# Attention's maxima pass starts 6 units ahead of the second pass instead of 20

## The chip, the cores and the metric

The kernel runs on one core of one Trainium2 chip. The core has five engines with queues of their own, TensorE (PE in the profile; PEld is its loading of weights), VectorE (DVE), ScalarE (ACT), GpSimd (POOL) and SyncE (SP), and 16 DMA engines. They run side by side and wait for each other on semaphores. The metric is the device time of one execution in microseconds.

## The reference

A block in float32 with a state space layer (two directions, 2 x 2048 tokens, 256 wide) and then a transformer block with causal attention (16 heads of 16) and a mixture of 8 experts. The change lies in the attention alone:

```
q, k = (rope(q), rope(k))
scores = jnp.einsum('bqhd,bkhd->bhqk', q, k) / math.sqrt(hd)
causal = jnp.tril(jnp.ones((Tt, Tt), dtype=bool))
scores = jnp.where(causal, scores, jnp.asarray(-1000000000.0, scores.dtype))
probs = jax.nn.softmax(scores, axis=-1)
attn = jnp.einsum('bhqk,bkhd->bqhd', probs, v).reshape(Bb, Tt, d) @ Wproj
```

with batch 2 and 2048 tokens in each sequence.

## The kernel before

The stages (`project_inputs`, `scan_channels`, `mix_and_qkv`, `attend`, `route`, `run_experts`, `combine`) run one after the other. Inside a stage each engine has its own program, written out in order, with waits on semaphores; nothing schedules them again.

`attend` works through 8 groups of four heads. A group's heads lie on four groups of 32 rows of TensorE, so four score matmuls can run at once. Each group goes through two passes over the causal half of its 2048 x 2048 scores.

The **first pass** finds the largest score of each query. Its piece of work is a *unit*: 128 queries against up to 512 keys, for four heads (`scores1`, line 1561, in two parts of two heads: heads 2 and 3, then 0 and 1). Each head's scores go into one of three PSUM banks (`S1 = 3`); VectorE reduces a bank to one maximum per query (`maxima`, line 1472), and only then is the bank free for the head three places later. 40 units make a group. A unit on the diagonal is narrower (384, 256, 128 or 0 whole columns and one triangle of 128) and ends in a reduction over the triangles (line 1482). A block of 512 queries is a *round*; rounds end with units 3, 11, 23 and 39. After the unit that follows, `turn_max` transposes the round's maxima on TensorE (line 1570, into the first of the three banks), VectorE copies them negated (line 1498), and SyncE writes them with four small DMAs (line 1400) into a spare row of the query tile, counted by `m_in`.

The **second pass** computes the scores again, the other way round, with the maxima subtracted by that extra row. Its piece of work is a *step*: 128 keys against 512 queries (fewer on the diagonal), for four heads, in two halves (`scores2`, line 1582). ScalarE takes the exponential (line 1532; lines 1535 to 1541 on the diagonal), GpSimd clears what lies above the diagonal (line 1438), and TensorE multiplies with the values (`values`, line 1602) one step later. A group has 40 steps; those on the diagonal (0 to 3, 8 to 11, 20 to 23, 36 to 39) are narrower. The first step of a round (0, 4, 12 and 24) waits for the round's `m_in`.

TensorE's program sets the order of both passes. Before step 0 it runs 20 units alone (`LEAD = 20`). Then each step carries one unit, 20 ahead of it: second-pass scores of two heads, first-pass scores of the two other heads, values, and the same again. The last 20 steps carry none.

Of the kernel before, what the change touches and what calls it, by code (L numbers as in the profile page):

```python
# [132 lines left out]
def hold(eng, k):  # L133


    eng.sem_inc(k["passed"], 1)
# [1187 lines left out]
def attend(nc, k, qk, va, attn, load_next):  # L1324
# [7 lines left out]
    GROUPS = B * H // HG  # L1332
    SETS = 2
    PB = 3
    LEAD = 20
    HALF = C // 2
    steps = [(qc, kt) for qc in range(NC) for kt in range(JT * qc + JT)]
    NSTEP = len(steps)


    units = []
    for qc in range(NC):
        whole = [(t, c) for t in range(JT * qc, JT * qc + JT) for c in range(qc)]
        crossed = [(t, qc) for t in range(JT * qc + JT - 1, JT * qc - 1, -1)]
        at = len(whole) if qc < NC - 1 else JT
        units += whole[:at] + crossed + whole[at:]
    assert len(units) == NSTEP
    NUNIT = GROUPS * NSTEP
    ends = [max(st for st, x in enumerate(steps) if x[0] == qc) for qc in range(NC)]
    S1 = 3  # L1350
    with Stage(nc, "attend") as s:
# [29 lines left out]
        @block.sync  # L1381
        def _(sp):
            sp.wait_ge(filled, 2 * SETS + 1)

            def load(n):
                if n >= SETS:
                    sp.wait_ge(s2_mm, (n - SETS + 1) * NSTEP * 2)
                b, g = n // (H // HG), n % (H // HG)
                for h in range(HG):
                    rows = slice((g * HG + h) * HD, (g * HG + h + 1) * HD)  # L1390
                    sp.dma_start(qt[n % SETS][head_rows(h), :], qk[b, 0, rows, :]).then_inc(loaded[n % SETS], 16)
                    sp.dma_start(kt_[n % SETS][head_rows(h), :], qk[b, 1, rows, :]).then_inc(loaded[n % SETS], 16)
                    sp.dma_start(qt[n % SETS][32 * h + HD:32 * h + HD + 1, :], zero[h:h + 1, :]
                                 ).then_inc(loaded[n % SETS], 16)

            def place_max(r):
                n, qc = r // NC, r % NC
                sp.wait_ge(m_rows, r + 1)
                for h in range(HG):
                    sp.dma_start(qt[n % SETS][32 * h + HD:32 * h + HD + 1, qc * C:(qc + 1) * C  # L1400
                                              ].rearrange("r (t q) -> r t q", q=P),
                                 mrows[h * JT:(h + 1) * JT, :]).then_inc(m_in, 16)

            load(0)
            for b in range(B):
                sp.dma_start(vall[:, b * KT:(b + 1) * KT, :, :].rearrange("p t h e -> p t (h e)"),
                             vav[:, b * KT:(b + 1) * KT, :]).then_inc(loaded_v[b], 16)
            for r in range(GROUPS * NC):
                if r % NC == 2 and r // NC + 1 < GROUPS:
                    load(r // NC + 1)  # L1410
                place_max(r)

            for i in range(2):
                sp.wait_ge(stored[i], 16 * NC * (H // HG) // 2)
            load_next(sp)

        @block.gpsimd
        def _(pool):
# [10 lines left out]
            for n in range(GROUPS):  # L1429
                b, g = n // (H // HG), n % (H // HG)  # L1430
                for st, (qc, kt) in enumerate(steps):
                    at = n * NSTEP + st
                    if kt < JT * qc:
# [14 lines left out]
        def round_after(u):  # L1448

            if u < 0 or u >= NUNIT or u % NSTEP not in ends:  # L1450
                return None
            return u // NSTEP * NC + ends.index(u % NSTEP)

# [91 lines left out]
        @block.tensor  # L1545
        def _(pe):
            pe.wait_ge(caps_ok, 1)

            def scores1(u, part):
                n, (t, c) = u // NSTEP, units[u % NSTEP]  # L1550
                if u % NSTEP == 0 and part == 0:
                    pe.wait_ge(loaded[n % SETS], (n // SETS + 1) * HG * 3 * 16)
                w = min(C, (t + 1) * P - c * C)
                for i, h in list(enumerate((2, 3, 0, 1)))[2 * part:2 * part + 2]:
                    v = u * HG + i
                    rows = slice(32 * h, 32 * h + 32)
                    if v >= S1:
                        pe.wait_ge(s1_read, v - S1 + 1)
                    if v % S1 == 0 and turned:
                        pe.wait_ge(m_rows, turned)  # L1560
                    pe.matmul(s1[v % S1][:, 0:w], qt[n % SETS][rows, t * P:(t + 1) * P],  # L1561
                              kt_[n % SETS][rows, c * C:c * C + w], start=True, stop=True).then_inc(s1_mm, 1)

            def turn_max(u, r):

                last = min(u + 1, NUNIT) * HG - 1
                pe.wait_ge(s1_read, last // S1 * S1 + 1)
                pe.wait_ge(m_ok, r + 1)
                hold(pe, k)
                pe.transpose(pm, m[:, :, :].rearrange("p h t -> p (h t)"), k["ident"][:, :]).then_inc(m_turned, 1)  # L1570

            def scores2(at, pair):
                n, (qc, kt) = at // NSTEP, steps[at % NSTEP]
                o = max(kt - JT * qc, 0) * P
                if kt == 0 and pair == 0:
                    pe.wait_ge(m_in, (n * NC + qc + 1) * HG * 16)
                if at:
                    pe.wait_ge(exp_ok, at * 2 - 1 + pair)
                for i in range(2):
                    h = 2 * pair + i  # L1580
                    rows = slice(32 * h, 32 * h + 32)
                    last = pe.matmul(s2[pair][:, i, o:], kt_[n % SETS][rows, kt * P:(kt + 1) * P],  # L1582
                                     qt[n % SETS][rows, qc * C + o:(qc + 1) * C], start=True, stop=True)
                last.then_inc(s2_mm, 1)

            def values(at, half):
                n, (qc, kt) = at // NSTEP, steps[at % NSTEP]
                b, g = n // (H // HG), n % (H // HG)
                o = max(kt - JT * qc, 0) * P
                if half == 0:  # L1590
                    pe.wait_ge(exp_ok, at * 2 + 2)
                    if kt >= JT * qc:
                        pe.wait_ge(kept_ok, n * KT + kt + 1)
                    if kt == 0:
                        pe.wait_ge(loaded_v[b], 16)
                        if n * NC + qc:
                            pe.wait_ge(pv_out, n * NC + qc)
                lo, hi = max(o, half * HALF), (half + 1) * HALF
                if lo >= hi:
                    return  # L1600
                for h in range(HG):
                    last = pe.matmul(pv[32 * h:32 * h + 32, lo:hi], vall[:, b * KT + kt, g * HG + h, :],  # L1602
                                     pb[at % PB][:, h, lo:hi], start=kt == 0 and half == 0,
                                     stop=kt == JT * qc + JT - 1, skip_group_check=True)
                if half == 1:
                    last.then_inc(pv_ok, 1)

            turned = 0
            for at in range(-LEAD, NUNIT):
                u = at + LEAD  # L1610
                if at >= 0:
                    scores2(at, 0)
                if u < NUNIT:
                    scores1(u, 0)
                    if at > 0:
                        values(at - 1, 0)
                if at >= 0:
                    scores2(at, 1)
                if u < NUNIT:
                    scores1(u, 1)  # L1620
                elif at > 0:
                    values(at - 1, 0)
                if at > 0:
                    values(at - 1, 1)
                if round_after(u - 1) is not None:
                    turn_max(u, round_after(u - 1))
                    turned += 1
            values(GROUPS * NSTEP - 1, 0)
            values(GROUPS * NSTEP - 1, 1)

# [709 lines left out]
```

## Time and profile before

| what | value |
|---|---|
| median of 3 runs | 4213.83 us (4213.8 to 4221.78) |
| span of the profiled execution, first to last instruction | 4222.2 us |
| TensorE busy | 3401.3 us, 81% of the span |
| VectorE busy | 2787.7 us, 66% |
| ScalarE busy | 2464.7 us, 58% |
| GpSimd busy | 1886.3 us, 45% |

The profile is of one execution, and gives no time of its own beside the span. It lies 8.4 us above the median and 0.4 us above the slowest of the runs. Busy times are unions of an engine's instructions; ends of matmuls are modelled. Attention runs from 2255.07 to about 3456 us of this span.

### The profile page before, as it was taken

How to read it: one execution, taken by the hardware profiler on the slowest of the kernel's cores; microseconds unless marked ns; L12 is line 12 of the kernel's file. 1: busy time of each engine (PE TensorE's matmuls, PEld its weight loads, DVE VectorE, ACT ScalarE, POOL GpSimd, SP SyncE). 2: the span in 40 equal slices, each digit the busy share in tenths (PEclk: the TensorE clock that was granted, in tenths of full speed). 3: DMA queues.
4: the chain of work that ended last, by engine and by line, in shares of the span. 5: the costliest groups of instructions: out<-in, count | busy, mean ns of one | idle time of the engine just before them, and what ended most of it. 6: DMA issues, size and time to landing. Idle time of an engine off the chain costs nothing. (4 is left out here: it accounts for less than half of the span.)

```text
span 4222.2 us, 69815 instructions
## 1 busy us (share of the span) xinstructions
PE 3401.3 (81%) x22940; PEld 2121.0 (50%) x22940; DVE 2787.7 (66%) x4369; ACT 2464.7 (58%) x3860; POOL 1886.3 (45%) x1761
## 2 busy tenths in 40 slices
PE   8567878878788787885876999999999976599980
PEld 4146666666666666664553333333333335366660
DVE  3258888888888888886764777777777727100105
ACT  3268888888888888884220555665566552122110
POOL 1048888888888888885541000010001015200006
PEclk9679999999999999998995999999999996799995
DMA  6533333333333333334634001011001025122205
GB/s 204 156 101 91 91 91 91 91 91 91 92 91 89 93 91 89 91 93 183 236 119 120 9 19 19 7 19 22 17 9 19 9 64 189 34 83 83 83 31 188
DMA packets 158040, 357.64 MB, mean 85 GB/s; under 512 B 20931, under 2 KB 65974, under 8 KB 143216
## 3 DMA queue, kind: packets, MB, share of 16 engines
q1 hardware_dynamic: 125392, 266.42, 22.8%
q0 software_dynamic: 16784, 52.10, 3.5%
q10 hardware_dynamic: 15504, 34.61, 2.2%
q8 instruction: 191, 3.13, 0.3%
q14 instruction: 169, 1.38, 0.1%
HBM read 253.24 MB, written 102.26 MB: 84 GB/s over the span
## 5 line engine op out<-in xcount | busy, mean ns | idle before, releaser
L506 POOL TENSOR_TENSOR scan_hC<-scan_hh,scan_cbc 128x512 f32<-128x512 f32 x1024 | 1382.8, 1379 | 160.1 <-DVE scan_hh L718 101.4
L718 DVE TENSOR_TENSOR_SCAN scan_hh<-scan_dA,scan_state,scan_bx 128x512 f32<-128x512 f32 x1024 | 1252.4, 1264 | 213.9 <-PE scan_bx L810 99.5
L810 PE MATMUL scan_bx<-kept_ident,scan_dBxT 128*128 128x128 f32 x4096 | 677.3, 292 | 197.5 <-DVE scan_hh L718 133.5
L1561 PE MATMUL attend_s<-attend_kt,attend_qt 32*128 32x512 f32 (+3 forms) x2560 | 793.7, 609 | 33.9 <-DMA attend_qt<-attend_zero 27.6
L559 ACT ACTIVATE scan_dBxT<-scan_dtxT,scan_bt 128x512 f32<-128x512 f32 x1028 | 655.7, 711 | 81.6 <-PE scan_bx L810 81.4
L820 PE MATMUL scan_acc<-kept_ident,scan_hC 128*128 128x128 f32 x4128 | 656.8, 287 | 56.1 <-ACT scan_uu L568 29.3
L810 PEld LDWEIGHTS scan_bx<-kept_ident,scan_dBxT 128*128 128x128 f32 x4096 | 502.4, 150 | 389.7 <-DVE scan_hh L718 232.1
L554 ACT ACTIVATE scan_dA<-scan_dt,scan_an 128x512 f32<-128x512 f32 x1028 | 660.9, 712 | 29.1 <-DVE scan_hh L718 29.1
L1582 PE MATMUL attend_s<-attend_qt,attend_kt 32*128 32x512 f32 (+3 forms) x2560 | 635.7, 581 | 17.9 <-POOL attend_pb L1438 14.6
L1472 DVE TENSOR_REDUCE attend_mx<-attend_s 128x1 f32<-128x512 f32 x768 | 494.5, 686 | 197.0 <-PE attend_s L1561 195.8
L1532 ACT ACTIVATE attend_pb<-attend_s 128x1024 f32<-128x1024 f32 x384 | 390.8, 1024 | 279.1 <-PE attend_s L1582 279.1
L820 PEld LDWEIGHTS scan_acc<-kept_ident,scan_hC 128*128 128x128 f32 x4128 | 517.1, 149 | 71.5 <-POOL scan_hC L506 38.2
L1438 POOL TENSOR_SCALAR_AFFINE_SELECT attend_pb<-attend_pb 128x512 f32<-128x512 f32 x128 | 81.4, 636 | 983.6 <-ACT attend_pb L1541 983.5
L1602 PE MATMUL attend_pv<-attend_pb,attend_vall 128*32 128x256 f32 (+1 forms) x4608 | 355.5, 383 | 31.1 <-POOL attend_pb L1438 29.9
L1561 PEld LDWEIGHTS attend_s<-attend_kt,attend_qt 32*128 32x128 f32 x2560 | 297.0, 192 | 115.1 <-DVE attend_mx L1472 44.1
L1582 PEld LDWEIGHTS attend_s<-attend_qt,attend_kt 32*128 32x128 f32 x2560 | 197.6, 185 | 260.9 <-issue 204.0
L1602 PEld LDWEIGHTS attend_pv<-attend_pb,attend_vall 128*32 128x32 f32 x4608 | 94.3, 108 | 412.9 <-issue 305.2
L2106 ACT ACTIVATE experts_hid<-experts_ph,weights_b1t 128x512 f32<-128x512 f32 x128 | 88.0, 687 | 335.7 <-PE experts_ph L2132 335.7
L1535 ACT ACTIVATE attend_below<-attend_s 128x256 f32<-128x256 f32 x256 | 98.4, 384 | 247.6 <-PE attend_s L1582 243.4
L1476 DVE TENSOR_REDUCE attend_mx<-attend_s 128x1 f32<-128x256 f32 (+2 forms) x384 | 160.3, 417 | 104.4 <-PE attend_s L1561 104.0
L2132 PE MATMUL experts_ph<-experts_xT,weights_w1t 128*128 128x512 f32 x512 | 223.6, 597 | 0.9 <-DVE experts_xT L2084 0.9
L2143 PE MATMUL experts_py<-weights_w2t,experts_hid 128*128 128x256 f32 x1024 | 222.3, 379 | 0.0
(207 smaller groups left out, 3675.1 us busy)
## 6 DMA issues: line engine op xcount, KB each, us to landing
scan_xs<-scratch_xin SPq DMA_DIRECT2D x288, 256.0 KB, 6.2
scan_cbc<-scratch_crows SPq DMA_DIRECT2D x64, 1024.0 KB, 4.8
scratch_y<-scan_uu ACTq DMA_DIRECT2D x17, 1024.0 KB
scratch_xin<-proj_out_x SPq DMA_DIRECT2D x8, 1024.0 KB
scratch_sz<-proj_out_z SPq DMA_DIRECT2D x8, 1024.0 KB
scratch_exp_in<-proj_cleared SPq DMA_DIRECT2D x8, 1024.0 KB, 8.4
mix_yf<-scratch_y SPq DMA_DIRECT2D x8, 1024.0 KB, 6.6
mix_yb<-scratch_y SPq DMA_DIRECT2D x8, 1024.0 KB, 9.5
```

The costliest lines, as they stand in the source:

```text
L506: pool.tensor_tensor(hC[n % 2][:, m, :], h[:, m, :], rows, ALU.mult).then_inc(hc_ok, 1)
L554: act.activation(dA[n % 2][:, m, :], dt[d][:, m, :], ACT.Exp, scale=an[:, d, m, n:n + 1]).then_inc(da_ok, 1)
L559: last = act.activation(dBxT[turned_slot(n)][:, j, :], dtxT[d][:, j, :], ACT.Copy, scale=bt[d][:, j, NS + n:NS + n + 1])
L718: dve.tensor_tensor_scan(hh[n % 2][:, m, r], dA[n % 2][:, m, r], bx[bank(j)][:, r], state[:, d, n, m:m + 1], ALU.mult, ALU.add).then_inc(h ...
L810: last = pe.transpose(bx[bank(j)][:, t * P:(t + 1) * P], dBxT[turned_slot(n)][:, t, m * P:(m + 1) * P], k["ident"][:, :])
L820: last = pe.matmul(acc[:, j, m * P:(m + 1) * P], hC[n % 2][:, m, j * P:(j + 1) * P], k["ident"][:, :], start=a == 0, stop=False, is_transp ...
L1472: dve.tensor_reduce(mx[:, h, t, c:c + 1], bank[:, :], AX_X, ALU.max).then_inc(s1_read, 1)
L1532: act.activation(own, score[:, :, :], ACT.Exp).then_inc(exp_ok, 1)
L1561: pe.matmul(s1[v % S1][:, 0:w], qt[n % SETS][rows, t * P:(t + 1) * P], kt_[n % SETS][rows, c * C:c * C + w], start=True, stop=True).then_i ...
L1582: last = pe.matmul(s2[pair][:, i, o:], kt_[n % SETS][rows, kt * P:(kt + 1) * P], qt[n % SETS][rows, qc * C + o:(qc + 1) * C], start=True, ...
L1602: last = pe.matmul(pv[32 * h:32 * h + 32, lo:hi], vall[:, b * KT + kt, g * HG + h, :], pb[at % PB][:, h, lo:hi], start=kt == 0 and half == ...
L2132: last = pe.matmul(ph[q % 2][:, :], w1t[e % 2][:, m, f * P:(f + 1) * P], xT[:, m, ch * C:(ch + 1) * C], start=m == 0, stop=m == KD - 1)
```

## The change

The first pass gets 6 units ahead before step 0, and the other 14 are put behind steps 0, 1, 2, 3 and then every second step up to step 22. From step 24 on the distance is 20 units again.

```
-    LEAD = 20
+    LEAD0 = 6
...
+    EXTRA = [1 if at < 4 or (at < 24 and at % 2 == 0) else 0 for at in range(GROUPS * NSTEP)]
...
-            for at in range(-LEAD, NUNIT):
-                u = at + LEAD
-                if at >= 0:
-                    scores2(at, 0)
+            u = 0
+
+            def close(u):
+                if round_after(u - 1) is not None:
+                    turn_max(u, round_after(u - 1))
+                    return 1
+                return 0
+
+            for u in range(LEAD0):
+                scores1(u, 0)
+                scores1(u, 1)
+                turned += close(u)
+            u = LEAD0
+            for at in range(NUNIT):
+                scores2(at, 0)
...
-                if round_after(u - 1) is not None:
-                    turn_max(u, round_after(u - 1))
-                    turned += 1
+                if u <= NUNIT:
+                    turned += close(u)
+                u += 1
+                for _ in range(EXTRA[at]):
+                    scores1(u, 0)
+                    scores1(u, 1)
+                    turned += close(u)
+                    u += 1
```

The steps then carry these units (two numbers where a step has an extra one): step 0: 6, 7; 1: 8, 9; 2: 10, 11; 3: 12, 13; 4: 14, 15; 5: 16; 6: 17, 18; 7: 19; 8: 20, 21; 9: 22; 10: 23, 24; 11: 25; 12: 26, 27; 13: 28; 14: 29, 30; 15: 31; 16: 32, 33; 17: 34; 18: 35, 36; 19: 37; 20: 38, 39; 21: 40; 22: 41, 42; 23: 43. Before, step n carried unit n + 20. No instruction is added or removed, and the other engines' own programs are the same text: they wait in the same order of units and of steps.

On TensorE, where the first pass alone ends. Before, after the first turn (line 1570) units 5 to 19 follow, of which the first six heads stand here; `s1` are the three banks of the first pass.

```order
L1570 MATMUL attend_s1_0<-kept_ident,attend_m 16x128
L1561 MATMUL attend_s1_2<-attend_kt0,attend_qt0 128x512
L1561 MATMUL attend_s1_0<-attend_kt0,attend_qt0 128x512
L1561 MATMUL attend_s1_1<-attend_kt0,attend_qt0 128x512
L1561 MATMUL attend_s1_2<-attend_kt0,attend_qt0 128x512
L1561 MATMUL attend_s1_0<-attend_kt0,attend_qt0 128x512
L1561 MATMUL attend_s1_1<-attend_kt0,attend_qt0 128x512
```

In the changed kernel (its lines are one higher) step 0 stands right behind unit 5; `s2` are the banks of the second pass.

```order
L1571 MATMUL attend_s1_0<-kept_ident,attend_m 16x128
L1562 MATMUL attend_s1_2<-attend_kt0,attend_qt0 128x512
L1562 MATMUL attend_s1_0<-attend_kt0,attend_qt0 128x512
L1562 MATMUL attend_s1_1<-attend_kt0,attend_qt0 128x512
L1562 MATMUL attend_s1_2<-attend_kt0,attend_qt0 128x512
L1583 MATMUL attend_s2_0<-attend_qt0,attend_kt0 128x512 x2
L1562 MATMUL attend_s1_0<-attend_kt0,attend_qt0 128x512
L1562 MATMUL attend_s1_1<-attend_kt0,attend_qt0 128x512
L1583 MATMUL attend_s2_1<-attend_qt0,attend_kt0 128x512 x2
```

Fourteen units have moved from ahead of the first second-pass scores to places behind them.

On TensorE, step 6, a full step, before: two score groups of the second pass with one unit's four heads, and the values of step 5.

```order
L1582 MATMUL attend_s2_0<-attend_qt0,attend_kt0 128x512 x2
L1561 MATMUL attend_s1_2<-attend_kt0,attend_qt0 128x512
L1561 MATMUL attend_s1_0<-attend_kt0,attend_qt0 128x512
L1602 MATMUL attend_pv<-attend_pb2,attend_vall 32x256 x4
L1582 MATMUL attend_s2_1<-attend_qt0,attend_kt0 128x512 x2
L1561 MATMUL attend_s1_1<-attend_kt0,attend_qt0 128x512
L1561 MATMUL attend_s1_2<-attend_kt0,attend_qt0 128x512
L1602 MATMUL attend_pv<-attend_pb2,attend_vall 32x256 x4
```

The same step in the changed kernel, up to the first rows of step 7:

```order
L1583 MATMUL attend_s2_0<-attend_qt0,attend_kt0 128x512 x2
L1562 MATMUL attend_s1_2<-attend_kt0,attend_qt0 128x512
L1562 MATMUL attend_s1_0<-attend_kt0,attend_qt0 128x512
L1603 MATMUL attend_pv<-attend_pb2,attend_vall 32x256 x4
L1583 MATMUL attend_s2_1<-attend_qt0,attend_kt0 128x512 x2
L1562 MATMUL attend_s1_1<-attend_kt0,attend_qt0 128x512
L1562 MATMUL attend_s1_2<-attend_kt0,attend_qt0 128x512
L1603 MATMUL attend_pv<-attend_pb2,attend_vall 32x256 x4
L1562 MATMUL attend_s1_0<-attend_kt0,attend_qt0 128x512
L1562 MATMUL attend_s1_1<-attend_kt0,attend_qt0 128x512
L1562 MATMUL attend_s1_2<-attend_kt0,attend_qt0 128x512
L1562 MATMUL attend_s1_0<-attend_kt0,attend_qt0 128x512
```

Four first-pass heads of the extra unit now stand between a step's last values and the next step's first scores.

On TensorE, the end of step 3 in the changed kernel, where round 1 is turned; before, this turn stood in the middle of the 20 units.

```order
L1583 MATMUL attend_s2_1<-attend_qt0,attend_kt0 128x128 x2
L1562 MATMUL attend_s1_2<-attend_kt0,attend_qt0 128x512
L1562 MATMUL attend_s1_0<-attend_kt0,attend_qt0 128x512
L1603 MATMUL attend_pv<-attend_pb2,attend_vall 32x256 x4
L1571 MATMUL attend_s1_0<-kept_ident,attend_m 16x128
L1562 MATMUL attend_s1_1<-attend_kt0,attend_qt0 128x512
L1562 MATMUL attend_s1_2<-attend_kt0,attend_qt0 128x512
L1562 MATMUL attend_s1_0<-attend_kt0,attend_qt0 128x512
L1562 MATMUL attend_s1_1<-attend_kt0,attend_qt0 128x512
L1583 MATMUL attend_s2_0<-attend_qt0,attend_kt0 128x512 x2
```

Only unit 13 stands between the turn of round 1 and step 4, which waits for its maxima.

## Rows read from the trace of the kernel before

**Rows 1.** Windows: us, each engine's busy time (instructions), granted clock, DMA share, GB/s.

```profile
2255.07:2278.20 23.13, 21.80 (x51) 10.43 (x52) 15.37 (x41) 0.00 (x0) 0.00 (x0) 0.50 0.94 347
2278.20:2330.69 52.49, 50.96 (x113) 25.66 (x112) 35.58 (x73) 0.00 (x0) 0.00 (x0) 0.50 0.16 21
2330.69:2415.94 85.25, 79.70 (x718) 30.92 (x717) 63.79 (x150) 51.33 (x92) 8.11 (x13) 0.96 0.02 8
2415.94:3403.00 987.06, 938.25 (x8411) 335.70 (x8410) 724.67 (x1589) 590.98 (x958) 84.71 (x137) 0.99 0.08 16
```

**Rows 2.** The page: one engine's busy time, and one group's busy us, mean ns, idle.

```profile
PE 3401.3 (81%) x22940; PEld 2121.0 (50%) x22940; DVE 2787.7 (66%) x4369; ACT 2464.7 (58%) x3860; POOL 1886.3 (45%) x1761
...
L1472 DVE TENSOR_REDUCE attend_mx<-attend_s 128x1 f32<-128x512 f32 x768 | 494.5, 686 | 197.0 <-PE attend_s L1561 195.8
```

**Rows 3.** Timeline (start, us, engine, line), the turn of round 0.

```profile
2273.51 0.38 PE L1570 MATMUL attend_s<-kept_ident,attend_m 128*16 128x128 f32 x1
...
2274.22 0.27 DVE L1498 TENSOR_SCALAR attend_mrows<-attend_s 16x128 f32<-16x128 f32 x1
2274.51 2.60 SPq L1400 DMA_DIRECT2D attend_qt<-attend_mrows  x4
...
2278.78 2.08 DVE L1472 TENSOR_REDUCE attend_mx<-attend_s 128x1 f32<-128x512 f32 x3 [0.78 <-PE attend_s L1561]
```

**Rows 4.** Windows of a microsecond each behind the turn of round 0.

```profile
2277.00:2278.00 1.00, 1.00 (x3) 0.66 (x3) 1.00 (x2) 0.00 (x0) 0.00 (x0) 0.50 0.02 4
2278.00:2279.00 1.00, 1.00 (x4) 0.50 (x2) 0.22 (x1) 0.00 (x0) 0.00 (x0) 0.50 0.00 0
```

**Rows 5.** Timeline, the first pass alone in its full units, and step 0.

```profile
2307.65 1.69 PEld L1561 LDWEIGHTS attend_s<-attend_kt,attend_qt 32*128 32x128 f32 x6 [1.85 <-DVE attend_mx L1472]
...
2310.50 1.69 PEld L1561 LDWEIGHTS attend_s<-attend_kt,attend_qt 32*128 32x128 f32 x6 [1.16 <-DVE attend_mx L1472]
...
2330.69 1.06 PE L1582 MATMUL attend_s<-attend_qt,attend_kt 32*128 32x512 f32 x1
```

**Rows 6.** Timeline of TensorE, first matmul of step 24.

```profile
2415.94 0.70 PE L1582 MATMUL attend_s<-attend_qt,attend_kt 32*128 32x512 f32 x2
```

**Rows 7.** Timeline, a plain full step.

```profile
2377.18 0.70 PE L1582 MATMUL attend_s<-attend_qt,attend_kt 32*128 32x512 f32 x2
...
2378.25 0.64 PE L1602 MATMUL attend_pv<-attend_pb,attend_vall 128*32 128x256 f32 x8
2378.40 1.29 DVE L1472 TENSOR_REDUCE attend_mx<-attend_s 128x1 f32<-128x512 f32 x2 [0.77 <-PE attend_s L1561]
...
2378.82 0.70 PE L1582 MATMUL attend_s<-attend_qt,attend_kt 32*128 32x512 f32 x2
...
2380.04 1.29 DVE L1472 TENSOR_REDUCE attend_mx<-attend_s 128x1 f32<-128x512 f32 x2 [0.35 <-PE attend_s L1561]
...
2380.76 0.70 PE L1582 MATMUL attend_s<-attend_qt,attend_kt 32*128 32x512 f32 x2
```

**Rows 8.** Timeline of VectorE, reads of a narrow unit.

```profile
2291.04 0.69 DVE L1482 TENSOR_REDUCE attend_mx<-attend_edge 128x4 f32<-128x512 f32 x1
...
2291.65 0.41 DVE L1476 TENSOR_REDUCE attend_mx<-attend_s 128x1 f32<-128x256 f32 x1
...
2292.18 0.41 DVE L1476 TENSOR_REDUCE attend_mx<-attend_s 128x1 f32<-128x256 f32 x1
```

**Rows 9.** Timeline of TensorE, the turn of round 2 between step 4 and step 5.

```profile
2349.32 0.43 PE L1602 MATMUL attend_pv<-attend_pb,attend_vall 128*32 128x128 f32 x8
...
2350.47 0.70 PE L1582 MATMUL attend_s<-attend_qt,attend_kt 32*128 32x512 f32 x2
```

**Rows 10.** Windows over steps 1, 3, 4 and 8 to 12.

```profile
2335.00:2340.00 5.00, 4.55 (x28) 1.85 (x26) 3.81 (x12) 3.12 (x8) 0.64 (x1) 0.80 0.02 5
2345.00:2350.00 5.00, 4.55 (x40) 1.70 (x40) 4.34 (x11) 3.32 (x6) 0.73 (x2) 1.00 0.00 0
2360.00:2380.00 20.00, 18.21 (x181) 6.75 (x176) 15.63 (x41) 13.35 (x28) 3.10 (x5) 1.00 0.03 9
```

More of the change, by code:

```diff
@@ L1616, in _ @@
                         values(at - 1, 0)
-                if at >= 0:
-                    scores2(at, 1)
+                scores2(at, 1)
                 if u < NUNIT:
```

## The prediction

> **What bounds the kernel now.** I first cut the attention stage into stretches [rows 1]. The reader should see three regimes. From 2255.07 to 2330.69 us, 75.6 us long, the first pass runs alone: ScalarE does nothing, TensorE has a granted clock of 0.50 (the 1.2 GHz level), and nothing of the second pass has started. From 2330.69 both passes run together at 0.96 to 0.99 (nearly always 2.4 GHz). TensorE is busy 79.7 of 85.25 us in the first 24 steps and 938 of 987 us after, VectorE 75% and 73%. TensorE is busy 81% of the whole span [rows 2]. So steady attention is bound by TensorE, and the lonely first pass by its round trip with VectorE. The change touches only the first and the start of the second regime; from step 24 on the distance between the passes is 20 units in both kernels, and everything there should only slide.
>
> **Gain: an earlier step 0.** The first six units stand as before. The turn of round 0 is behind unit 4: TensorE transposes at 2273.51, VectorE copies at 2274.22, SyncE issues four small writes from 2274.51 [rows 3]. Step 0 needs their landing. The core's DMA share is 0.02 in the microsecond before 2278 and 0.00 after it [rows 4], so they have landed by then (the 8 MB of values loaded ahead of them on the same queue too). The eighth head of units 4 and 5 is read at 2278.78 [rows 3], so its matmul is done about then. I take 2278.5 for step 0; it was 2330.69 [rows 5]. The shift is 52.2 us; bounds are 50 (landing late by 2 us) and 52.7.
>
> **Cost: 14 units inside steps 0 to 23.** Those steps took 2330.69 to 2415.94 [rows 5, 6], 85.25 us. None of the old extra time is free cover, because the fourteen units need the same two engines.
>
> A plain full step lasts 3.58 us, from 2377.18 to 2380.76 [rows 7]. Its first half: a group of four score matmuls on the four row groups (two of the second pass, two heads of a unit) 1.07, values 0.57. VectorE starts to read 1.22 after the group starts and reads a head each 0.645 us; a bank is free 0.69 after its read starts [rows 2, 7]. The second half starts at 1.64 and lasts 1.94, since its second unit head waits for a bank.
>
> Now an extra unit behind it. There are three banks, so each head waits for the read three heads back. Times from the step's start: heads 1 to 4 are read at 1.22, 1.87, 2.86, 3.50. Head 5 starts when values end, 3.58, and is read at 4.80. Head 6 is read at 5.45. Head 7 starts at 4.2 (bank of head 4), is read at 6.10, bank free 6.80. Head 8 waits for head 5's bank, 5.5, and is read at 6.75. TensorE takes instructions in order, so the next step stands behind head 8; its own two unit heads need the banks of heads 6 and 7, free at 6.15 and 6.80. The next step's group ends as if it had begun at 6.80. That is 3.2 more than 3.58; the next step's second half then has its banks in time and gets 0.3 back. So an extra full unit costs 2.9 us.
>
> Nine of the fourteen are full: 9 x 2.9 = 26.1. The narrow ones read faster (a 256-column unit each 0.53 us) but end in a 0.69 us reduction [rows 8]; the same reckoning gives 2.4 for the two of 256, 1.9 for the two of 128 and 1.3 for the one without columns: 9.9. Sum 36.0.
>
> Bounds of this price: if the unit cost only VectorE's own time, a step with two units would last 8 x 0.65 = 5.2, 1.6 more than 3.58: 14 x 1.6 = 23 us. If it cost what it costs alone in the old prologue, where three heads take 2310.50 - 2307.65 = 2.85 us [rows 5], it would be 3.8 us each: 53 us. I stay with 36, which lies between and uses the durations of the full clock.
>
> Further terms, each small:
> - Step 0 and 1 run at 1.2 GHz at first, as before; the extra unit of step 0 costs about 1 more there.
> - Wide units now meet narrow steps (steps 3 and 11 had units of 0 columns): two times 0.85, together 1.7.
> - Turns. From transpose to landing is 4.5 us [rows 3, 4]. Round 1 is turned at the end of step 3, and only unit 13 lies between it and step 4, which waits for it: about 8.5 us after step 3's start instead of 7.0, so 1.5 lost. Round 2 is turned behind the extra unit of step 10: TensorE waits for that unit's last read (1.1), and step 12 waits 0.6 more. The old kernel turned round 2 at step 4, with 0.7 to 0.8 us between values and the next group [rows 9]; that goes away. Sum +2.4. Behind each such wait stand the second-pass scores, and ScalarE's exponentials behind those. SyncE's queue: the loads for group 1 move with the turn of round 1 and are not waited for until unit 40.
> - Clock. After step 0 the granted clock was 0.80 in 2335 to 2340 and 1.00 from 2345 [rows 10]. Extra steps lie between the lonely first pass (0.50) and plain steps (1.00). While the extra unit runs, TensorE has only its heads. I allow 8 us at the lower level, at half a microsecond lost each: 4 us. Bounds are 0 and the rival below.
>
> The Trainium skill, TensorE: Matmul & The Clock Gate, section "A second HAM failure mode: psum-queue depth-cycling", says that a kernel which cycles through PSUM buffers leaves TensorE short idles between groups of matmuls, and that its clock then swings between the levels. The prologue here, three banks in turn, agrees as far as it goes: 0.50 all along. By that rule the sum would be the third rival's.
>
> **Sum.** -52.2 + 36.0 + 1.0 + 1.7 + 2.4 + 4 = -7.1 us. The profiled execution's span is 4222.2 us, 8.4 above the median 4213.83 and at the upper edge of the runs shown; stretches of attention should not differ by more than the clock's swings, so I take the difference from the median: **4207 us** (on the profiled span 4215). A measurement here tells about 0.2%, 8.4 us, from no change: the forecast is within it, near its edge.
>
> **Rivals.**
> 1. *VectorE alone sets the price* of an extra unit, 23 us, because TensorE runs ahead on the banks better than I reckon. With the other terms except the clock (5.1): -52.2 + 28 = -24, 4190 us. For it: VectorE is idle a quarter of the steady time [rows 1]. Against: the bank order above follows from the rows of a plain step, where the second half already loses 0.3.
> 2. *The units cost as much as before*, 3.6 to 3.8 us each: nothing gained; -52.2 + 53 = about 0 to +1, 4214 us. For it: a round trip, not work, set the prologue. Against: at the full clock that trip is 1.22 and not the 2.1 of the prologue (2.85 less a read).
> 3. *Slower: the clock stays down.* Place: the steps with an extra unit. At 1.2 GHz the same reckoning (group 2.1, values 1.1, trip 2.1) makes such a step 11.2 us instead of 6.8, 4.4 more. Without the 4 us allowance the change stands at -11.1; so it decides from two and a half such steps on, and from five on the kernel is slower by over 0.2%. With seven: -11.1 + 31 = +20, 4234 us. For it: 0.50 while the first pass ran alone, 0.80 after step 0. Against: the stretch 2360 to 2380, with the narrow steps 9 to 11 and TensorE idle 1.8 us, kept 1.00 [rows 10], and 0.96 is the mean of all 24 [rows 1].
>
> **How the numbers follow.** The forecast has 0.50, spread over 4200 to 4214: two fifths of that, 0.20, below 4205.4, the rest within 0.2%. VectorE's price 0.20, all faster. As dear as before 0.17: 0.15 within, 0.02 slower. The clock 0.13: 0.10 slower, 0.03 within. So faster 0.40, within 0.2% 0.48, slower 0.12. The range, 8 in 10, goes from the first rival to just past the second: 4189 to 4220. The likeliest case's own range is 4200 to 4214.
>
> **What would show it.** Step 0's first second-pass matmul (line 1582 before, 1583 after) near 2278.5 instead of 2330.69 on the attention's own clock. From it to step 24 about 130 us instead of 85. A step with two full units near 6.8 us; step 3 near 8.5 with a wait for the maxima. From step 24 on the same spacing as before. It is wrong if a double step lasts 5.3 (first rival) or over 8 (second and third; the granted clock between step 0 and 24 tells which), or if step 0 waits long for the four writes.

## The result and the profile after

The changed kernel is slower: 1.0025 times the time of before, 95% interval 1.0017 to 1.0033, with medians of 4230.0 us against 4217.2 us (9 runs each; the three runs shown ahead are among those of before). Forecast was 7 us less; by the ratio it is about 10.5 us more (the two medians lie 12.9 us apart). The measured 4230 us lie above the range given, 4189 to 4220.

The windows of the changed kernel, cut where those of before were [rows 1]: the first pass alone, steps 0 to 23, and the rest of attention.

```profile
2250.90:2274.00 23.10, 21.81 (x49) 9.76 (x50) 15.37 (x41) 0.00 (x0) 0.00 (x0) 0.50 0.93 342
2274.00:2419.91 145.91, 139.61 (x828) 55.90 (x827) 100.15 (x223) 51.54 (x92) 8.73 (x14) 0.77 0.07 12
2419.91:3472.00 1052.09, 1000.77 (x8888) 360.05 (x8884) 727.23 (x1593) 630.77 (x1028) 89.51 (x145) 0.97 0.09 18
```

Up to step 0 it is 23.10 us instead of 75.6; forecast was 23.4. Steps 0 to 23 take 145.91 us instead of 85.25; forecast was 130.3. The column behind GpSimd's says why to look at the clock: 0.77 granted, against 0.96. With only two levels, 0.77 means that (1 - 0.77) / 0.5 x 145.91, some 67 us, were at 1.2 GHz; before it was 7 us. The same stretch cut near where the level changes (from 2349 to 2380 it changes several times; the last window ends 4 us behind step 24's start):

```profile
2274.00:2288.00 14.00, 13.66 (x72) 7.00 (x72) 11.27 (x26) 5.12 (x12) 1.27 (x2) 0.87 0.00 1
2288.00:2322.00 34.00, 32.89 (x144) 12.75 (x146) 18.38 (x39) 8.31 (x16) 1.84 (x3) 0.50 0.25 40
2322.00:2349.00 27.00, 24.39 (x191) 9.88 (x183) 21.44 (x51) 12.07 (x25) 1.90 (x3) 1.00 0.01 2
2349.00:2380.00 31.00, 30.05 (x167) 10.32 (x170) 18.80 (x46) 10.34 (x12) 1.19 (x2) 0.67 0.03 9
2380.00:2410.00 30.00, 29.19 (x208) 11.35 (x205) 23.81 (x44) 13.18 (x22) 1.26 (x2) 1.00 0.00 1
2410.00:2424.00 14.00, 13.52 (x74) 6.32 (x72) 8.29 (x26) 3.77 (x10) 1.27 (x2) 0.52 0.01 1
```

The clock falls in three spells. TensorE's busy column doesn't tell them apart: 32.89 of 34 us at the lower level, 29.19 of 30 at the full one. ScalarE's points the same way, with 8.3 us of exponentials in 34 us against 13.2 in 30, but steps 2 and 3, which lie in the first of these spells, are narrow and have less for it to do.

Extra units at the full clock, TensorE's timeline: the last values ahead of the extra units of steps 16, 18 and 20, and what follows the first.

```profile
2380.84 0.64 PE L1603 MATMUL attend_pv<-attend_pb,attend_vall 128*32 128x256 f32 x8
2381.41 2.60 PE L1562 MATMUL attend_s<-attend_kt,attend_qt 32*128 32x512 f32 x7
...
2390.79 0.64 PE L1603 MATMUL attend_pv<-attend_pb,attend_vall 128*32 128x256 f32 x8
...
2400.73 0.64 PE L1603 MATMUL attend_pv<-attend_pb,attend_vall 128*32 128x256 f32 x8
```

From one to the next is an extra unit and two steps, 9.95 and 9.94 us. Two plain steps are 7.16 [rows 7], so the unit costs 2.8 us there. Step 4, with an extra unit at the lower level, and the first scores of step 5:

```profile
2302.98 1.21 PE L1583 MATMUL attend_s<-attend_qt,attend_kt 32*128 32x512 f32 x1
...
2311.97 1.22 PE L1583 MATMUL attend_s<-attend_qt,attend_kt 32*128 32x512 f32 x1
```

9.0 us for that one step, against 3.58 + 2.8 at the full clock.

Step 0's wait, in the timeline and in the list of who waited for whom on the loading of weights (us in total, times, longest), steps 0 to 23:

```profile
2274.00 0.29 PEld L1583 LDWEIGHTS attend_s<-attend_qt,attend_kt 32*128 32x128 f32 x2 [1.03 <-DMA attend_qt<-attend_mrows]
```

```profile
PEld attend_s L1583 <- DMA attend_qt<-attend_mrows: 1.6, 2, 1.0
```

The second pass waits 1.6 us in all for maxima on their way, 1.0 at step 0 and 0.6 at step 4. The transfers are not where the time went.

From step 24 to the end of attention the program is the same, yet this profile has 1052 us against 1042 in the same window of before:

```profile
2415.94:3457.86 1041.92, 988.49 (x8888) 355.42 (x8884) 726.92 (x1593) 632.49 (x1029) 90.34 (x146) 0.99 0.09 19
```

What that is worth, the experiments show.

### The profile page after: what moved, and what is told of

The parts are those of the page before. It is cut to its first block and busy times, and to the rows that moved or that the text cites. A ratio compares the mean times of both kernels' runs of the same rounds, so it can differ in the third digit from the quotient of the medians.

```text
span 4228.1 us, 69815 instructions
## 1 busy us (share of the span) xinstructions
PE 3415.8 (81%) x22940; PEld 2123.1 (50%) x22940; DVE 2794.9 (66%) x4369; ACT 2463.5 (58%) x3860; POOL 1886.8 (45%) x1761
## 3 DMA queue, kind: packets, MB, share of 16 engines
q1 hardware_dynamic: 125392, 266.42, 22.7%
## 5 line engine op out<-in xcount | busy, mean ns | idle before, releaser
L1562 PE MATMUL attend_s<-attend_kt,attend_qt 32*128 32x512 f32 (+3 forms) x2560 | 803.9, 612 | 38.4 <-DMA attend_qt<-attend_zero 28.7
L1583 PE MATMUL attend_s<-attend_qt,attend_kt 32*128 32x512 f32 (+3 forms) x2560 | 663.0, 597 | 14.8 <-POOL attend_pb L1439 12.5
L1603 PE MATMUL attend_pv<-attend_pb,attend_vall 128*32 128x256 f32 (+1 forms) x4608 | 364.9, 392 | 28.5 <-POOL attend_pb L1439 27.7
L1583 PEld LDWEIGHTS attend_s<-attend_qt,attend_kt 32*128 32x128 f32 x2560 | 210.0, 192 | 260.5 <-issue 216.0
```

## Experiments

Two theories. *Clock*: the extra steps bring the granted clock down; that, and not their work, is what the forecast missed. *Round trip*: an extra unit costs some 4.2 us by its trips through three banks at any clock, and the low clock is only seen beside it. In the table, "alone" is the time from attention's first matmul to step 0, "steps" that from there to step 24's first matmul, each with its granted clock; the ratio is to the kernel before.

| run | units ahead, extra steps | alone, us (clock) | steps, us (clock) | ratio, 95% interval |
|---|---|---|---|---|
| before | 20, 0 | 75.6 (0.50) | 85.25 (0.96) | 1 |
| changed | 6, 14 | 23.1 (0.50) | 145.9 (0.77) | 1.0025 (1.0017 to 1.0033) |
| e0_changed_again | 6, 14 | 23.1 (0.50) | 153.3 (0.71) | 1.0039 (1.0027 to 1.0050) |
| e1_filled_steps | 6, 14 | 23.1 (0.50) | 130.5 (0.93) | 0.9994 (0.9985 to 1.0003) |
| e2_every_second | 8, 12 | 29.9 (0.50) | 142.5 (0.76) | 1.0030 (1.0018 to 1.0041) |
| e4_filled_prologue | 20, 0 | 61.4 (0.86) | 82.6 (1.00) | 0.9963 (0.9949 to 0.9976) |
| e5_all_filled | 6, 14 | 22.7 (0.71) | 132.6 (0.90) | 0.9982 (0.9974 to 0.9991) |
| e6_waits_only | 6, 14 | 23.1 (0.50) | 146.1 (0.77) | 1.0020 (1.0008 to 1.0032) |
| e7_lead10 | 10, 10 | 37.4 (0.50) | 131.5 (0.80) | 1.0030 (1.0020 to 1.0040) |
| e8_wide_filling | 20, 0 | 59.5 (0.92) | 82.6 (1.00) | 0.9959 (0.9943 to 0.9975) |

**e0_changed_again**: the changed kernel, no edit.

> The changed kernel once more, for the spread of its trace. In its first profile steps 0 to 23 took 144.8 us (step 0's first matmul to step 23's last exponential) with 66 us at the lower clock level, and groups 1 to 6 together took about 9 us more than in the kernel before, with 44 instead of 17 us at the lower level. Clock theory (the extra steps bring the granted clock down and that is what the forecast missed): 138 to 150 us with 50 us or more at the lower level in steps 0 to 23; groups 1 to 6 fall back towards the kernel before, since nothing in them was moved, and their excess is chance. Rival (something that the change leaves behind slows the later groups too): groups 1 to 6 are again 5 us or more dearer. Time 4225 to 4235 us.

Steps 0 to 23 are at 0.71 and 153.3 us, above the range given, as is the median, 4237.3 us. Steps 0 to 23 and the rest of attention:

```profile
2275.75:2429.05 153.30, 146.76 (x829) 59.93 (x828) 100.58 (x223) 51.62 (x92) 8.73 (x14) 0.71 0.06 12
2429.05:3481.58 1052.53, 998.30 (x8888) 357.92 (x8884) 726.45 (x1593) 631.52 (x1028) 89.51 (x145) 0.98 0.08 18
```

1052.5 us again, so from these two alone the rival stood. But the kernels that don't move the units have 1041.9 (before), 1050.8 (e4) and 1048.0 (e8) there, and those that do have 1045.9 (e2) to 1053.5 (e5). The time goes with the clock: by the clock's records in the traces 24 us of the stretch were at the lower level in the kernel before, 36 in e2, 41 in e8, 51 in e4, 55 in the changed kernel and 59 in e5, and a straight line through all ten profiles gives 0.33 us more for each us at that level. The 1042 of before was a low one, and only one profile of it exists; whether the move adds to the time at the lower level behind step 24 is not shown.

**e1_filled_steps**: beside each extra unit, scores that nobody needs.

```
+            def again(at, pair):
...
+                pe.wait_ge(exp_ok, at * 2 + 1 + pair)
+                for i in range(2):
+                    h = 2 * pair + i
+                    rows = slice(32 * h, 32 * h + 32)
+                    pe.matmul(s2[pair][:, i, o:], kt_[n % SETS][rows, kt * P:(kt + 1) * P],
+                              qt[n % SETS][rows, qc * C + o:(qc + 1) * C], start=True, stop=True)
...
                 for _ in range(EXTRA[at]):
+                    again(at, 0)
                     scores1(u, 0)
+                    again(at, 1)
                     scores1(u, 1)
```

> The changed kernel; beside each extra unit TensorE computes the step's own second-pass scores again into their bank, after ScalarE has read them, on the row groups that stand idle there. More work, no other order of waits. Clock theory: the lower level shrinks from 66 us to under 25 us in steps 0 to 23, which take 125 to 135 us instead of 144.8; time 4205 to 4220 us. Rival (the extra unit costs 4.2 us whatever the clock, by its round trip through the three banks): steps 0 to 23 take 144 us or more, time 4230 us or more.

```profile
2275.83:2406.28 130.45, 124.19 (x941) 54.08 (x940) 100.24 (x223) 51.55 (x92) 8.76 (x14) 0.93 0.08 14
```

TensorE records 941 matmuls instead of 828, VectorE and ScalarE do the same work, and the stretch is 15.5 us shorter at 0.93. More work took less time, because the clock stayed up. The round trip theory falls. 130.45 is close to the forecast's 130.3, and it had allowed about as much time at the lower level (18 us here, 15 there). Stretch, time at the lower level and median (4217.6 us) all lie in the ranges given. The time of the whole is that of before, 0.9994.

**e6_waits_only**: the same without the two `pe.matmul` lines, so only the added waits.

> The filled steps' control: the changed kernel with the waits of the filling (for ScalarE's two exponentials of the step, ahead of the two halves of an extra unit) and without its matmuls. Clock theory: the filling worked by its matmuls, so this behaves as the changed kernel: 50 us or more at the lower level in steps 0 to 23, which take 140 us or more; time 4225 to 4240 us. Rival (the waits put the instructions into a better order and that was the gain): steps 0 to 23 take 125 to 135 us, time 4212 to 4220 us.

```profile
2278.25:2424.39 146.14, 140.73 (x828) 56.20 (x827) 100.22 (x223) 51.60 (x92) 8.75 (x14) 0.77 0.07 12
```

As the changed kernel, to the digit of the clock, and within the ranges given (4231.4 us). The matmuls did it, not the waits.

**e2_every_second** and **e7_lead10**: fewer extra units, spread out.

```
+    LEAD0 = 8
+    EXTRA = [1 if at < 24 and at % 2 == 0 else 0 for at in range(GROUPS * NSTEP)]
```

```
+    LEAD0 = 10
+    EXTRA = [1 if 4 <= at < 24 and at % 2 == 0 else 0 for at in range(GROUPS * NSTEP)]
```

> 8 units ahead and one extra unit in every second step of the first 24 (12 of them), none in two steps running. Step 0 starts about 45 us earlier than in the kernel before. Clock theory: plain steps between keep the clock up for most of the stretch, an extra unit costs 2.9 to 3.5 us: steps 0 to 23 take 122 to 130 us; time 4205 to 4217 us. Rival (4.2 us each at any clock): 136 us or more, time 4221 us or more.

> 10 units ahead, extra units only behind steps 4, 6, ... 22 (10 of them): none in the narrow steps 0 to 3, and the turn of round 1 is not squeezed. Clock theory: the extra steps still bring the clock down, 40 us or more at the lower level in steps 0 to 23, which take 125 to 138 us; with step 0 about 37 us earlier than in the kernel before that gives 4220 to 4232 us. Rival (the fall of the clock began in the crowded steps 0 to 4 with the wait for round 1's maxima): under 20 us at the lower level, steps 0 to 23 take 112 to 118 us, time 4207 to 4214 us.

```profile
2283.76:2426.24 142.48, 134.78 (x813) 53.83 (x811) 96.07 (x217) 51.57 (x92) 8.72 (x14) 0.76 0.06 12
```

```profile
2292.74:2424.25 131.51, 125.56 (x799) 49.79 (x798) 90.40 (x203) 51.51 (x92) 8.74 (x14) 0.80 0.07 13
```

For e2 I had expected that plain steps between the extra ones keep the clock up. They don't: 0.76, with 142.5 us and a median of 4231.8 us, both in the rival's ranges. The price per extra unit over plain steps is (142.5 - 85.25) / 12 = 4.8 us, near the rival's 4.2, but the rival has that price at any clock, and by e1 it is the clock's doing. e7 shows that the crowded steps 0 to 4 and their wait for round 1 are not needed for the fall: none of them has an extra unit, and the clock is at 0.80, the price 4.6. Its stretch lies in the range given; its time, 4234.6 us, is a little above.

**e4_filled_prologue** and **e8_wide_filling**: the kernel before, with the first pass filled in the same way.

```
+            def twice(u, part):
...
+                w = min(C, (t + 1) * P - c * C)
...
+                for i in range(2):
+                    h = 2 * part + i
+                    rows = slice(32 * h, 32 * h + 32)
+                    pe.matmul(s2[part][:, i, 0:w], qt[n % SETS][rows, t * P:(t + 1) * P],
+                              kt_[n % SETS][rows, c * C:c * C + w], start=True, stop=True)
...
+                if at < 0:
+                    twice(u, 0)
                 if u < NUNIT:
                     scores1(u, 0)
...
+                if at < 0:
+                    twice(u, 1)
                 if u < NUNIT:
                     scores1(u, 1)
```

In e8 the repeats are always 512 columns wide (`s2[part][:, i, :]`, no `w`).

> The kernel before, 20 units ahead; in the first pass alone TensorE computes each unit's scores a second time, into the still unused banks of the second pass, on the row groups that stand idle. Clock theory: the stretch before step 0, 75.6 us at 1.2 GHz, goes to 2.4 GHz for most of its time and takes 54 to 60 us, bound by VectorE; time 4196 to 4204 us. Rival (the round trip with VectorE sets it at any clock, or the clock doesn't rise): 73 us or more; time 4213 us or more.

> The kernel before with the first pass filled by full 512-column repeats for every unit, narrow ones too (the first filling used the unit's own width, and the clock fell for some 17 us around the narrow units). Clock theory: at most 8 us at the lower level before step 0, reached after 56 to 60 us (61.4 with the narrow filling, 75.6 with none); time 4198 to 4204 us. Rival (the narrow units are bound by the wider repeats themselves): 62 us or more, time 4204 us or more.

Windows of e4 (alone; steps 0 to 23; the rest) and VectorE's timeline in its full units:

```profile
2251.82:2313.18 61.36, 58.23 (x321) 37.10 (x322) 50.79 (x114) 0.00 (x0) 0.00 (x0) 0.86 0.49 149
2313.18:2395.76 82.58, 76.80 (x718) 29.57 (x717) 63.93 (x150) 51.34 (x92) 8.12 (x13) 1.00 0.02 8
2395.76:3446.53 1050.77, 998.88 (x8888) 359.35 (x8884) 727.47 (x1593) 632.30 (x1029) 90.43 (x146) 0.98 0.09 18
```

```profile
2298.46 2.60 DVE L1472 TENSOR_REDUCE attend_mx<-attend_s 128x1 f32<-128x512 f32 x4 [0.18 <-PE attend_s L1561]
2301.24 2.60 DVE L1472 TENSOR_REDUCE attend_mx<-attend_s 128x1 f32<-128x512 f32 x4 [0.18 <-PE attend_s L1561]
2304.01 2.60 DVE L1472 TENSOR_REDUCE attend_mx<-attend_s 128x1 f32<-128x512 f32 x4 [0.18 <-PE attend_s L1561]
```

and of e8:

```profile
2254.27:2313.80 59.53, 57.54 (x322) 35.31 (x322) 50.81 (x114) 0.00 (x0) 0.00 (x0) 0.92 0.51 153
2313.80:2396.37 82.57, 76.84 (x719) 29.63 (x717) 63.97 (x150) 51.27 (x92) 8.09 (x13) 1.00 0.02 8
2396.37:3444.38 1048.01, 995.58 (x8888) 358.47 (x8884) 727.97 (x1593) 631.67 (x1029) 90.16 (x146) 0.98 0.09 19
```

A unit alone takes 2301.24 - 2298.46 = 2.78 us, of which VectorE reads 2.60; before, at 0.50, it was 3.8. e4 missed its range up to step 0 by 1.4 us, and its time, 4204.1 us, stands at the edge. e8 keeps the clock at 0.92 (9.5 us at the lower level, where I had said at most 8) and is 1.8 us shorter there, a difference that the ratios can't tell. Both are faster than the kernel before and than the changed one, with the old order and with each unit's scores computed twice in the first pass.

**e5_all_filled**: the changed kernel with `again` beside its extra units and `twice` beside its six first ones.

> The changed kernel with both fillings: each extra unit beside repeated second-pass scores, and the six units ahead of step 0 beside repeated scores of their own. It asks what the move itself is worth once the clock is up on both sides; its partner is the kernel before with a filled first pass, which took 61.4 us up to step 0 and 82.8 us for steps 0 to 23, together 144.2 us, at 0.9963 of before. Clock theory (at 2.4 GHz a unit costs 2.8 us alone and 2.9 us in a step, so the move is worth nothing): 19 to 23 us up to step 0 and 125 to 130 us for steps 0 to 23, together 145 to 152 us; time 4201 to 4212 us, not below the partner. Rival (units behind steps are half hidden once the clock is up): together under 138 us, time under 4198 us.

```profile
2254.14:2276.80 22.66, 19.86 (x97) 12.20 (x97) 15.96 (x42) 0.00 (x0) 0.00 (x0) 0.71 0.95 353
2276.80:2409.43 132.63, 127.61 (x939) 56.53 (x939) 99.18 (x222) 51.61 (x92) 8.63 (x14) 0.90 0.08 13
```

155.3 us up to step 24, against 143.9 in e4 and 142.1 in e8: above the 145 to 152 that I gave. Its median, 4214.2 us, is above the range too, and its ratio, 0.9982 (0.9974 to 0.9991), lies above that of e8, 0.9959 (0.9943 to 0.9975), from the same chip; the intervals only touch. But the filling did not hold the clock here: some 13 us of the first stretch and 27 of the second were at the lower level, against 9.5 and none in e8. So this run doesn't show what the move is worth with the clock up on both sides. An estimate takes 0.24 us per us at that level in the first pass alone ((75.6 - 59.5) over the 66 us by which before and e8 differ) and 0.33 in the steps: 143 us against 140, so the move would be worth nothing, or a little less. Against the kernel before, which has none of the filling, this one is faster by the filling, not by the move.

## Why the prediction was wrong

- **The earlier step 0 was right.** 52.2 us were forecast; 75.62 - 23.10 is 52.5. The four writes landed about when they were expected, and step 0 waited 1.0 us for them.
- **The price of a unit at the full clock was right.** 2.9 us were reckoned, 2.8 us stand in the timeline. VectorE's price (first rival, 1.6) is nowhere seen. The turns of the rounds were no trouble: 1.6 us of waiting for the maxima. The count was off by one: of the fourteen extra units ten are full, two have 256 whole columns, one 128 and one none, which makes 37.0 us and not 36.0. (The second rival's sum has a slip as well: it leaves out the small terms of 5.1 us that the first has in; with them it stands at +6, 4220 us.)
- **The clock's term is the step that failed.** "I allow 8 us at the lower level, at half a microsecond lost each: 4 us." It was 60 us more than before, and the stretch is 145.9 - 126.3 = 19.6 us over the forecast without that term (18.6 with the count put right). So there was seven times as much time at the lower level as allowed, and the loss per microsecond of it is about 0.33, less than the half. Three other runs of the moved units give about the same over the same 126.3: e0 27 us for 81 more at that level, e6 19.8 for 60, e5 6.3 for 20. That it is less than the half fits with VectorE's reads of a bank, which take about as long at either level (0.69 us at 0.50 [rows 3], 0.65 at 1.00 [rows 7]). With 19.6 in place of 4 the sum is +8.5 us; the profiles give 169.0 - 160.9 = +8.1 up to step 24, the runs about 10.5. The forecast's time also stood on a median of three runs, 4213.8 us, where nine runs gave 4217.2: 3 us of the miss are no error of the mechanism.
- **The third rival is what happened**, to which I gave 0.13. Its mechanism is shown by e1 with e6: nothing but useless matmuls on idle row groups brought steps 0 to 23 from 145.9 to 130.5 us. Its size and its place were off. Its price was too high (4.4 us more for an extra step at 1.2 GHz, 11.2 in all; step 4 at that level took 9.0 from its first scores to step 5's), and it put the whole loss on seven extra steps. In the trace only the extra units of steps 2, 3, 4 and 22 ran wholly at the lower level; the rest of the 67 us fell on other work of the steps.
- **The argument that I weighed against it was the wrong one.** The stretch 2360 to 2380 of before kept its clock with TensorE idle for 1.8 us, and I took that as a sign that extra steps would too. But an extra unit is not idle time in the busy column: TensorE has one pass's matmuls and no other, as in the first pass alone, which is 51 of 52.5 us busy and at 0.50 [rows 1]. The nearer row was there, and I had used it for the gain only.

The Trainium skill, TensorE: Matmul & The Clock Gate, section "A second HAM failure mode: psum-queue depth-cycling", tells of a kernel whose cycling through PSUM banks left TensorE short idles between groups of matmuls, and whose clock swung between the levels. The trace agrees on the swing: 0.50, 1.00, 0.67, 1.00 and 0.52 in turn between step 2 and step 24. The idles don't show in its busy column, which has 32.89 of 34 us in the first of these spells.

What a unit costs or saves sums it up. Taken out of the first pass at 0.50 it saves 52.5 / 14 = 3.75 us. Put behind steps it costs (145.9 - 85.25) / 14 = 4.3 us with the clock falling, 3.2 in e1 with the clock mostly held. With the first pass filled in both kernels (e4 and e5, some 17 and 13 us of it at the lower level) the same fourteen units give back only (61.36 - 22.66) / 14 = 2.8. The first pass alone takes 75.6 us at 0.50 and 59.5 at 0.92: 16 us of it were the clock's. The rest, some 2.8 us a unit, is nearly all VectorE's reading, and a unit put behind a step at the full clock costs as much.

What stays open: which property of the added matmuls kept the clock up, since the filling adds matmuls and fills row groups at once; why the clock fell around some extra units and stayed up at others (those of steps 16 and 18); why e5, with both fillings, still spends some 27 us of steps 0 to 23 at the lower level (0.90); and how much of the 10.5 us lies behind step 24, where single profiles of one program differ by as much.

## What to carry to other kernels

A stretch that runs one of two passes alone can be slow because its engine is at the lower clock, and moving work out of it into a dense stretch can take the low clock along. Before moving work, ask what a stretch would take at the full clock. Its time multiplied by its granted clock is the least that this can be (here 75.6 x 0.50 = 37.8 us), and the share that other engines set stays (VectorE is busy for 51 us of it; 59.5 were measured at 0.92). Here raising the clock gained time, and the move lost some. And read the clock's column beside the busy column: the second can be full where the first is at half.

## What the runs showed of the hardware

- Matmuls whose results nobody reads made the kernel faster: 0.9963 and 0.9959 of before, by 0.86 and 0.92 of granted clock in place of 0.50 in the first pass alone.
- TensorE was busy 32.9 of 34 us by the profile and stayed at 1.2 GHz all that time; the same engine, 29.2 of 30 us busy, was at 2.4 GHz two spells later in the same kernel.
- Attention behind step 24, the same program in all kernels, took from 1041.9 to 1053.5 us in ten profiles, with 0.97 to 0.99 granted. The time follows the clock, at 0.33 us for each us at the lower level (24 to 59 us of it), and not at the half that the clock's ratio alone would give.
